# Wavelet-conv block with a median blur: the median's steps reordered, GpSimd's work tied to steps of the median, two images no longer done in halves, and a shorter run of filler matmuls

## The reference, cut to what matters

```python
# layer 0
cA, cH, cV, cD = dwt2(x)                           # Haar bands, 16x16 each
rimg0 = idwt2(*[bn_relu(conv1x1(c, conv_w)) for c in (cA, cH, cV, cD)])
rimg1 = idwt2(...)                                 # 3 levels down and back up: equals x
y = conv3x3(concat([rimg0, rimg1], channels), convW_w) + convW_b
y = bn_relu(y, bnW_gamma, bnW_beta)                # batch statistics over all 16 images
# layer 1
m = median_blur(y, 3)                              # 3x3 median of each channel, zero padding
out = y + conv1x1(m, L1_W) + L1_b
```

## Time and profile before

| | |
|---|---|
| Three runs | 433.34, 434.85, 435.02 us |
| The profiled execution | 433.21 us |
| Its span in the trace | 431.4 us, so 1.8 us lie around it |
| PE matmul busy | 403.5 us (94%), 1150 instructions |
| DVE busy | 400.2 us (93%), 532 instructions |
| POOL, ACT busy | 201.6 us (47%), 148.7 us (34%) |
| Granted TensorE clock, mean | 0.988 of full speed |

### The profile page before, as it was taken

How to read it: one execution, slowest core, us unless ns; L and a number is a source line. 1 busy time by engine, 2 the same in 40 slices (tenths; PEclk the granted TensorE clock), 3 DMA queues, 4 the chain that set the end, 5 groups by cost and what they waited for, 6 DMA issues and landing times.

```text
span 431.4 us, 3699 instructions
## 1 busy us (share of the span) xinstructions
PE 403.5 (94%) x1150; PEld 212.9 (49%) x1150; DVE 400.2 (93%) x532; ACT 148.7 (34%) x342; POOL 201.6 (47%) x191
## 2 busy tenths in 40 slices
PE   7887999999999999999999999999999969678895
PEld 2333698855444444444444444444455858553332
DVE  3899739999789999999999999999999999999996
ACT  2546742404141322222233314142323312217922
POOL 4999391707181917264453627180826600003630
PEclk9999999999999999999999999999999998969999
DMA  8960200101010101010101001010100000000566
GB/s 306 418 273 1 99 0 2 49 0 47 4 49 0 49 2 49 0 49 0 50 1 49 12 36 50 0 49 0 51 0 0 0 1 2 0 0 0 242 258 281
DMA packets 7652, 26.72 MB, mean 62 GB/s; under 512 B 976, under 2 KB 1232, under 8 KB 7504
## 3 DMA queue, kind: packets, MB, share of 16 engines
q1 hardware_dynamic: 7632, 26.48, 16.0%
HBM read 18.09 MB, written 8.39 MB: 61 GB/s over the span
## 4 chain that ended last, share of the span: by engine, by line
DVE 71%; PE 23%; issue 3%; DMA 1%; ACT 0%; SPq 0%; DVEq 0%
PE conv_ps L359 19%; DVE one_ps L724 4%; DVE sorted_cols L760 4%; DVE one_ps L772 4%; DVE one_ps L774 4%; DVE sorted_cols L768 4%; DVE one_ps L758 4%; DVE z L776 4%; DVE sorted_cols L729 4%; DVE sorted_cols L727 4%; DVE sorted_cols L731 4%; DVE sorted_cols L726 4%; DVE sorted_cols L770 3%; DVE sorted_cols L766 3%; DVE y L854 3%
## 5 line engine op out<-in xcount | busy, mean ns | idle before, releaser
L359 PE MATMUL conv_ps<-ru,wt 128*128 128x512 f32 (+1 forms) x360 | 132.4, 505 | 0.0
L359 PE MATMUL conv_ps<-xu,wt 128*128 128x496 f32 (+3 forms) x240 | 89.8, 512 | 11.5 <-DVE conv_ps L702 11.5
L359 PEld LDWEIGHTS conv_ps<-ru,wt 128*128 128x128 f32 x360 | 69.7, 194 | 53.4 <-issue 49.7
L533 ACT ACTIVATE y<-conv_ps,sgn 128x512 f32<-128x512 f32 (+1 forms) x40 | 25.7, 642 | 185.1 <-PE conv_ps L359 185.1
L278 POOL TENSOR_TENSOR xu<-raw 128x480 f32<-128x480 f32 x16 | 16.7, 1042 | 138.3 <-PE conv_ps L359 138.3
L359 PEld LDWEIGHTS conv_ps<-xu,wt 128*128 128x128 f32 x240 | 46.6, 195 | 48.2 <-issue 33.2
L359 PE MATMUL conv_ps<-y,v 128*128 128x496 f32 (+3 forms) x120 | 43.8, 501 | 1.6 <-ACT wt L486 1.6
L359 PE MATMUL conv_ps<-y,wt 128*128 128x496 f32 (+3 forms) x120 | 43.7, 500 | 0.0
L359 PE MATMUL conv_ps<-ru,v 128*128 128x496 f32 (+3 forms) x120 | 43.7, 500 | 0.0
L341 PE MATMUL one_ps<-y,w 128*128 128x512 f32 x64 | 30.2, 610 | 5.3 <-DVE z L611 3.8
L433 PE MATMUL conv_ps<-z,w 128*128 128x512 f32 x64 | 30.3, 612 | 4.0 <-DVE y L854 4.0
(11 more groups left out here) (124 smaller groups left out, 669.2 us busy)
## 6 DMA issues: line engine op xcount, KB each, us to landing
raw<-x SPq DMA_DIRECT2D x20, 512.0 KB, 3.3
out<-y SPq DMA_DIRECT2D x15, 512.0 KB, 2.7
ru<-x SPq DMA_DIRECT2D x8, 512.0 KB, 8.6
xu<-x SPq DMA_DIRECT2D x4, 512.0 KB, 8.6
wt<-w_t SPq DMA_DIRECT2D x1, 1152.0 KB, 11.3
out<-y SPq DMA_DIRECT2D x2, 256.0 KB, 2.8
w<-w_t SPq DMA_DIRECT2D x2, 64.0 KB, 4.6
vec<-vectors SPq DMA_DIRECT2D x1, 3.0 KB, 9.3
```

The lines of the kernel that those rows point to most:

```text
L359: return nc.tensor.matmul(bank(u, b)[:, (r0 - row) * BW:(r1 - row) * BW], taps(half, kx, ky), plane[:, (r0 + dy) * BW:(r1 + dy) * BW], sta ...
L533: S.activation(at(slot(n), row * W + b, [[2, cols]]), src, ACT.Identity, scale=sgn[:, :], accum_out=y_sum[:, part:part + 1]).then_inc(y_ke ...
```

## The change

`BRIDGE` goes from 30 to 16. `HALVED` holds images 0 and 15 alone, so there are 18 units. `BN3_AT` and `FINISH_AT` have new counts, with nine finishes inside the last two pieces and not twelve.

The median still has 18 instructions of the same sizes, the same six of them with two inputs in SBUF. Their order and their buffers differ: instruction 10 writes to `z` and not to `col_lo`, 13 is now `min(dense, highs)` into `col_lo`, 14 and 16 make `col_hi` with 15 (`max` into `dense`) between them. Instructions 2 and 12 are counted on their own semaphores, `rows_read` and `mids_read`, and no longer on `dve_done`, so `after(back)` and the counts of `place` pass over them. The seeding of unit u + 2 stands behind instruction 12 where the piece belongs to a halved image; in a whole image its first half stands between 16 and 17, and its second between 17 and 18. Of the waits for the instruction directly in front only two are left, of 17 for 16 and of 18 for 17, and in a whole image the seeding stands between these. The wait for `med_made` moves from the end of a piece to instruction 4 of the next.

POOL's order for image n becomes `ru12`, `ru03`, `xu03`. For n > 3, `ru12` waits for `mids_read` of image n - 3. `xu03(n)` waits for `rows_read` of image n - 2.

```diff
-    WARM_UP, KEEP_WARM, BRIDGE = 8, 24, 30
+    WARM_UP, KEEP_WARM, BRIDGE = 8, 24, 16
-    BN3_AT, FINISH_AT = 9, (19, 20, 22, 24, 25, 27, 28, 30, 31, 32, 34, 35)
-    SEED_AT = 12
+    BN3_AT, FINISH_AT = 8, (17, 18, 20, 21, 22, 24, 25, 27, 28)
-    HALVED = (0, 1, IMAGES - 2, IMAGES - 1)
+    HALVED = (0, IMAGES - 1)
...
             for n in range(2, IMAGES):
+                if n > 3:
+                    pool.wait_ge(mids_read, last_unit(n - 3) + 1)
                 pool.wait_ge(bands_normed, n + 1)
                 pool.wait_ge(q_done, last_unit(n - 2) + 1)
                 pool.wait_ge(ru03_made, n - 1)
                 make_ru12(G, n).then_inc(ru12_made, 1)
+                make_ru03(n)
+                pool.wait_ge(rows_read, last_unit(n - 2) + 1)
                 make_xu03(n)
-                make_ru03(n)
...
+                early, late = (seeds, None) if n in HALVED else (None, seeds)
...
                 step(V.tensor_tensor(sorted_rows(0), even, odd, ALU.min))
-                step(V.tensor_tensor(sorted_rows(HALF), even, odd, ALU.max))
-                after(1)
+                V.tensor_tensor(sorted_rows(HALF), even, odd, ALU.max).then_inc(rows_read, 1)
+                after()
                 step(V.tensor_tensor(cols(col_mid), twice(0), third, ALU.max))
+                if n > 0:
+                    dve.wait_ge(med_made, n)
                 step(V.tensor_tensor(cols(col_lo), twice(0), third, ALU.min))
-                after(2)
+                dve.wait_ge(rows_read, kept // 2)
...
                 step(V.tensor_tensor(dense3, both(0), outer(col_lo), ALU.max))
-                after()
-                step(V.tensor_tensor(padded(col_lo), both(HALF), outer(col_hi), ALU.min))
+                after(1)
+                step(V.tensor_tensor(at(zslot(n), r0 * W, [[W, nr], [2, BW], [1, 2]]), both(HALF), outer(col_hi), ALU.min))
                 after(1)
                 step(V.tensor_tensor(p1, pair(col_mid, 0), pair(col_mid, 1), ALU.min))
                 after(1)
-                step(V.tensor_tensor(p2, pair(col_mid, 0), pair(col_mid, 1), ALU.max))
-                after()
+                V.tensor_tensor(p2, pair(col_mid, 0), pair(col_mid, 1), ALU.max).then_inc(mids_read, 1)
+                if early is not None:
+                    seed_even(early)
+                    seed_odd(early)
+                after(1)
+                step(V.tensor_tensor(body(col_lo), dense, highs(), ALU.min))
+                dve.wait_ge(mids_read, kept // 2)
                 step(V.tensor_tensor(padded(col_hi), both(HALF), outer(col_mid), ALU.min))
-                after()
+                after(1)
+                step(V.tensor_tensor(dense, dense, highs(), ALU.max))
+                after(1)
                 step(V.tensor_tensor(padded(col_hi), both(0), padded(col_hi), ALU.max))
-                step(V.tensor_tensor(body(col_mid), dense, body(col_lo), ALU.min))
-                after()
-                step(V.tensor_tensor(dense, dense, body(col_lo), ALU.max))
+                if late is not None:
+                    seed_even(late)
                 after()
                 step(V.tensor_tensor(dense, dense, body(col_hi), ALU.min))
+                if late is not None:
+                    seed_odd(late)
                 after()
-                return V.tensor_tensor(at(zslot(n), r0 * W, [[W, nr], [1, W]]), dense, body(col_mid), ALU.max)
+                return V.tensor_tensor(highs(), dense, body(col_lo), ALU.max)
```

More of the change, by code:

```diff
@@ L150, in wavelet_conv_median_kernel @@
         ru03_made = sem("ru03_made")
+        rows_read = sem("rows_read")
+        mids_read = sem("mids_read")
         xu03_made = sem("xu03_made")
@@ L693, in _, with seed_even @@
             make_ru12(V, 1).then_inc(ru12_made, 1)
-            def seed(u):
+            def seed_even(u):
                 cols = UNITS[u][2] * BW
@@ L701, in seed, with seed_odd, median @@
                 V.tensor_tensor(p_bank, p_kept[u % 2][:, 0:cols], q_bank, ALU.add)
+            def seed_odd(u):
+                cols = UNITS[u][2] * BW
+                q_bank = conv_ps[:, u % 2, BANK:BANK + cols]
                 V.tensor_tensor(q_bank, p_kept[u % 2][:, 0:cols], q_bank, ALU.subtract).then_inc(seeded, 1)
-            def median(n, kept, pair0=0, pairs=BH, step=step):
+            def median(n, kept, pair0=0, pairs=BH, step=step, seeds=None):
+                early, late = (seeds, None) if n in HALVED else (None, seeds)
                 r0, nr = 2 * pair0, 2 * pairs
@@ L720, in cols, with highs @@
                     return at(t, r0 * PITCH + 1, [[2 * PITCH, pairs], [PITCH, 2], [1, W]])
+                def highs():
+                    return at(zslot(n), r0 * W, [[W, nr], [1, W]])
                 step(V.tensor_tensor(sorted_rows(0), even, odd, ALU.min))
-                step(V.tensor_tensor(sorted_rows(HALF), even, odd, ALU.max))
-                after(1)
+                V.tensor_tensor(sorted_rows(HALF), even, odd, ALU.max).then_inc(rows_read, 1)
+                after()
                 step(V.tensor_tensor(cols(col_mid), twice(0), third, ALU.max))
+                if n > 0:
+                    dve.wait_ge(med_made, n)
                 step(V.tensor_tensor(cols(col_lo), twice(0), third, ALU.min))
-                after(2)
+                dve.wait_ge(rows_read, kept // 2)
                 step(V.tensor_tensor(cols(col_hi), twice(HALF), third, ALU.max))
@@ L752, in median @@
                 dense = at(tmp2, 0, [[W, nr], [1, W]])
-                after(1)
+                after(2)
                 step(V.tensor_tensor(p1, pair(col_lo, 0), pair(col_lo, 1), ALU.max))
@@ L785, in _, with medians @@
                 done_pairs = upto
-            def medians(pieces, step=step):
+            def medians(pieces, step=step, seeds=None):
                 for n, pair0, pairs, u in pieces:
-                    ins = median(n, 2 * (u + 1), pair0, pairs, step)
+                    ins = median(n, 2 * (u + 1), pair0, pairs, step, seeds)
                     if pair0 + pairs == BH:
                         ins.then_inc(med_made, 1)
-                        dve.wait_ge(med_made, n + 1)
                     else:
                         step(ins)
[L795 to L809, removed]
+            for u in range(2):
+                seed_even(u)
+                seed_odd(u)
             dve.wait_ge(sgn_ready, 1)
@@ L816, in _ @@
             for u in range(len(UNITS) - 2):
-                medians(PIECES[u:u + 1], seeding(u + 2))
+                medians(PIECES[u:u + 1], seeds=u + 2)
             def second_batch_norm():
```

## The result

The changed kernel takes 430.85 us (median of six runs, 429.58 to 431.79) against 434.71 us (six runs too): ratio 0.9915, interval 0.9893 to 0.9937. Forecast was 430.4 us, faster.

The account below looks back on a forecast made before the run. PE and DVE run level at about 20.17 us per image, DVE's medians setting the end. Statistics over at 386.0 + close 37.7 + 3.3 = 427.0 span; 428.8 with 1.8 around it; 1.64 more gives 430.4 us, range 426.5 to 434.5.

Parts of the forecast that it names:

- part 5: End of the middle: last seeding done at 375.2, last outputs 7.0 us, second statistics over at 386.0 against 391.32.
- part 6: The close after the second statistics: 37.7 us against 36.8, with 1.2 us more waits among the last finishes.
- Part 1: DVE's median order: a direct wait costs 0.12 us, six go per whole median, 0.7 us saved.
- rival A's first form: DVE stays the bound because direct waits are not shortened: 433.7 us, no change; rival A as a whole 0.14.
- Part 2: POOL's new order and waits: its meeting with DVE costs 1.1 us per median; DVE waits about 0.6 us per image.
- Part 3: Seeding later in whole images, done 17.4 us into the median: free in the middle.
- Part 4: Shorter filler bridge in the opening: outputs(0) starts at 55.9 against 58.64, 2.7 us earlier.
- Rival D: The opening does not follow the bridge, 0 and not 2.7 us: 433.1 us, no change; chance 0.06.
- Rival B: PE stays at 1.2 GHz after its 11.5 us wait, 8.3 us more in last outputs and filler: 436.9, slower; chance 0.08.

Follow-up runs that it names:

- x3: Changed kernel with six instructions of each median (9, 10, 13 to 16) waiting for the one directly in front: 432.81 us, ratio 0.9967.
- x2: Changed kernel with 30 filler matmuls in the bridge again and not 16: 433.19 us, ratio 0.9984.
- x7: Changed kernel with twelve finishes inside the last two medians and not nine: 428.3 us, ratio 0.987.
- x4: Changed kernel with POOL's earlier order (ru12, xu03, ru03) and without its waits for rows_read and mids_read: 432.86 us, ratio 0.9969.
- x11: Changed kernel with last seeding at instruction 12 of image 14's median, twelve finishes, POOL's last two ru03 held until rows are sorted: 423.55 us, ratio 0.9764.
- x1: The changed kernel unaltered, timed once more: 430.77 us, ratio 0.9926 to the kernel before.
- x5: Changed kernel with the last seeding at instruction 12 of image 14's median, not behind 16 and 17: 426.55 us, ratio 0.9837.

## Why the prediction was right

The sign and the mechanism came out as forecast: DVE with time to spare in every image, one long wait of PE, one of DVE, a longer close. The size did in the main, but that 430.4 meets 430.85 so closely is in part luck. For the profiled execution the sum gave a span of 427.0 us, and it was 428.7: 0.2 us too little for PE's release and 0.8 for the last outputs (part 5), 0.7 for the close (part 6). Then the sum added 1.64 us, by which the median of before lay above its profiled execution; after the change this is 430.85 - 430.46 = 0.4 us. The two errors, 1.7 too little and 1.2 too much, nearly cancel. Between the profiled executions the change won 433.21 - 430.46 = 2.75 us where 4.4 were forecast.

- Part 1, the order: 0.12 us per direct wait, confirmed by x3, which also refutes rival A's first form. Here a next instruction does start earlier when it need not wait: 1.13 us after the one in front, whose own time is 1.22. So the measurement decides against the rule of the Trainium skill ("VectorE: DVE Perf Modes", "The DRAIN you can't avoid") that the prediction weighed, by which the semaphore costs nothing. The same section also says that a next operation that isn't held starts earlier, and with that the trace agrees.
- Part 2, POOL: 1.1 us taken for the meeting, 1.0 measured. DVE's wait was 0.68 for "about 0.6".
- Part 3, the later seeding: free in the middle, as forecast. PE's only wait for a seeding is the last one.
- Part 4, the bridge: 2.7 forecast, 2.6 in the trace, 2.4 by x2. Rival D is out. The prediction's 5.07 us for a halved block is the right number, but the end of the filler in the earlier trace rows is 47.09 + 6.64 = 53.73 and not 53.6.
- Part 5: PE was let go at 375.39 (forecast 375.2) after 11.3 us (11.5). The mis-sized term is the last outputs, 7.0 us taken from the earlier trace rows and 381.94 + 1.27 - 375.39 = 7.8 measured, since the clock stood lower for longer:

```profile
375.30:380.30 5.00, 4.91 (x12) 3.97 (x13) 5.00 (x11) 0.00 (x0) 0.00 (x0) 0.50 0.00 0
380.30:383.40 3.10, 3.07 (x14) 2.58 (x14) 0.03 (x1) 1.11 (x4) 0.00 (x0) 0.92 0.00 0
```

  The columns are those of the earlier trace rows, and the third number from the end is the granted clock: 0.50, that is 1.2 GHz, for five us, then nearly back. Rival B named this mechanism; of the 8.3 us that it gave it, 0.8 came.
- Part 6, the close: 37.7 forecast, 38.4 measured. The 2.3 us of waits for `mix` are exactly there, but before they were 0.9 us and not the 1.1 of the sum, which explains 0.2 of the 0.7; the rest is not traced. x7 shows that they and more can be had back.
- What the prediction saw but did not say: it added up parts of both signs without a line for each. Part 5 has the cost of the whole image 14 in it (DVE's idle 3.4 us and PE's 11.5 are its marks), and a sum for the halved image would have shown that this edit loses 2.4 us. Worth of the parts and time of the whole are two questions; only the second was answered.

## What to carry to other kernels

Where one engine sets the pace of a loop, time saved on the other turns into waiting, one for one, except in the last rounds: 0.7 us saved in each of 14 medians moved PE's last release by 1.7 us and the end by 2.0, from the last two. What pays on the second engine is the place of its last hand-over. Moving one seeding up by five instructions in one image won about 4 us, as much as this whole change.

## What was not expected of the hardware

- After a wait of 4.6 to 13 us, PE's last outputs (24 records, 5.07 us at full clock) took from 6.7 (x4) and 7.03 us (before) to 8.1 (x2). The length of the wait doesn't order them: 7.7 us after 4.6 (x11), 6.7 after 12.5 (x4). With the same program from `outputs(0)` up to them they took 7.45 (x7), 7.8, 8.0 (x1) and 8.1 us (x2), so this moves the end by up to 0.6 us.
- The opening scatters more. `outputs(0)` starts at 56.07 in the changed kernel and at 57.09 in x1, the same program, and 1.0 of the 1.1 us between their spans lies ahead of it. It is there after 12 us already: PE's second group of eight matmuls starts at 10.96 and at 12.04, both at a granted clock of 1.00, while the inputs are being loaded. Why is open.
- These two may make the changed kernel's spread of 2.2 us. Against it, x11, in which DVE does not wait for the last outputs but which has the same opening, spreads over 0.35 us only (423.24 to 423.59, five executions).
- One execution of x5 took 2398 us. In its trace PE is busy for 2390 us, and six matmul records of 512 columns take 15.5 us from start to start where 2.5 is usual, from the first filler on, with a granted clock of 1.00. No other of the study's runs shows it, and its cause is open.
